# Macaron layers on one core: routing weights of a first-layer expert slot spread by one DMA instead of two, and the first group's spreading moved from the setup into the first pass

## What is computed

```
x = x + 0.5 * L0_ffn(layernorm(x))      # 16 experts of 64, 4 taken, and a shared expert
x = x + L0_attn(layernorm(x))           # causal softmax attention, 16 heads of 8
x = x + 0.5 * L0_ffn(layernorm(x))
x = x + 0.5 * L1_ffn(layernorm(x))      # 8 experts of 256, 2 taken
x = x + L1_attn(layernorm(x))           # gated, in blocks of 64, with a linear part
x = x + 0.5 * L1_ffn(layernorm(x))
```

```
h1 = einsum('td,eid->tei', xf, w1)
h3 = einsum('td,eid->tei', xf, w3)
h = silu(h1) * h3
y = einsum('tei,edi,te->td', h, w2, comb)    # comb[t, e]: the routing weight, 0 where not taken
```

## Time and profile before

| what | us |
|---|---|
| median of 3 runs | 1778.22 |
| lowest, highest | 1775.87, 1778.82 |
| the profiled execution, its own time | 1777.67 |
| its span in the trace | 1775.7 |

### The profile page before, as it was taken

The page is one execution under the profiler, slowest core; times in us unless marked ns, Lnnn a source line. Parts: engine busy times, 40 slices in busy tenths (PEclk is TensorE's granted clock), DMA queues, the critical chain, the costliest instruction groups (busy, mean ns, idle before and its releaser), DMA issues. The chain is left out here.

```text
span 1775.7 us, 25917 instructions
## 1 busy us (share of the span) xinstructions
PE 1644.0 (93%) x8360; PEld 1149.7 (65%) x8360; DVE 1289.3 (73%) x3879; ACT 1016.6 (57%) x1718; POOL 774.5 (44%) x734
## 2 busy tenths in 40 slices
PE   3999879899999999998999999999998988999998
PEld 2777645555555555554777767777777876777776
DVE  4777668788778878883777767777766876767775
ACT  3666415565566566566666645555555645555554
POOL 1566611311311311212566646555574615555555
PEclk9999969999999999999999999999999998999999
DMA  4222211011111111101233332111110002111120
GB/s 149 74 91 84 93 33 35 16 24 25 21 30 24 20 22 28 30 11 38 79 121 120 103 95 88 54 49 48 49 48 1 1 1 90 60 55 60 55 94 19
DMA packets 58246, 95.01 MB, mean 54 GB/s; under 512 B 9312, under 2 KB 17120, under 8 KB 58112
## 3 DMA queue, kind: packets, MB, share of 16 engines
q1 hardware_dynamic: 56000, 91.07, 18.2%
q10 hardware_dynamic: 2112, 2.30, 0.4%
HBM read 76.76 MB, written 2.88 MB: 45 GB/s over the span
## 5 line engine op out<-in xcount | busy, mean ns | idle before, releaser
L695 DVE TENSOR_TENSOR big<-banks,big 128x512 f32<-128x512 f32 x384 | 264.4, 689 | 214.7 <-ACT banks L632 179.8
L1157 ACT ACTIVATE big<-banks 128x1024 f32<-128x1024 f32 (+3 forms) x384 | 304.3, 810 | 187.9 <-PE banks L1068 182.5
L632 ACT ACTIVATE banks<-banks 128x512 f32<-128x512 f32 x384 | 224.0, 583 | 277.3 <-PE banks L575 272.1
L705 DVE TENSOR_TENSOR big<-big,banks 128x512 f32<-128x512 f32 x400 | 274.7, 687 | 29.8 <-PE banks L578 15.9
L1049 PE MATMUL banks<-arena 128*128 128x512 f32 (+3 forms) x768 | 251.9, 407 | 32.2 <-DVE att_mx L1285 15.4
L1285 DVE CUSTOM_DVE_ANT_0 banks<-banks,att_mask 128x128 f32<-128x128 f32 (+3 forms) x512 | 235.6, 521 | 52.2 <-PE banks L1049 51.6
L1197 POOL TENSOR_SCALAR_AFFINE_SELECT big<-big 128x512 f32<-128x512 f32 x128 | 81.2, 635 | 402.5 <-ACT big L1157 402.5
L1049 PEld LDWEIGHTS banks<-arena 128*128 128x128 f32 x768 | 136.6, 199 | 162.3 <-issue 98.2
L665 POOL TENSOR_TENSOR ffn1b_hid_l<-big,ffn1b_hid_h 128x512 fp32r<-128x512 f32 x128 | 165.5, 1293 | 128.3 <-ACT ffn1b_hid_h L637 128.3
L665 POOL TENSOR_TENSOR ffn1a_hid_l<-big,ffn1a_hid_h 128x512 fp32r<-128x512 f32 x128 | 165.2, 1291 | 118.0 <-ACT ffn1a_hid_h L637 118.0
L575 PE MATMUL banks<-xh,arena 128*128 128x512 f32 x512 | 208.7, 408 | 7.9 <-PEq L1451 6.8
(11 more groups left out here) (256 smaller groups left out, 3153.7 us busy)
## 6 DMA issues: line engine op xcount, KB each, us to landing
big<-weight_rows SPq DMA_DIRECT2D x256, 128.0 KB, 3.0
big<-weight_rows SPq DMA_DIRECT2D x128, 256.0 KB, 4.3
arena<-att_parts SPq DMA_DIRECT2D x16, 384.0 KB
arena<-att_parts SPq DMA_DIRECT2D x128, 48.0 KB
w_raw<-in_ffn_w_dram SPq DMA_DIRECT2D x12, 256.0 KB, 3.0
out_dram<-x SPq DMA_DIRECT2D x8, 256.0 KB, 2.3
setup_raw<-in_ffn_w_dram SPq DMA_DIRECT2D x3, 576.0 KB, 6.9
gau_angle<-in_consts_dram SPq DMA_DIRECT2D x2, 512.0 KB, 7.3
```

Source lines behind the costliest of these rows:

```text
L632: act.activation(gate if c < NSCALED else sil, gate, ACT.Silu).then_inc(silu_done, 1)
L695: dve.tensor_tensor(scl[:, num % 2, :], gate_ps[:, num % NB, :], share[:, c // PER, :], ALU.mult)\
L705: dve.tensor_tensor(hid[:, num % NH, :], scl[:, num % 2, :] if c < NSCALED else sil, up_ps[:, num % NB, :], ALU.mult).then_inc(hidden, 1)
L1157: act.activation(probs[:, unit % NPROB, 2 * pair:2 * pair + 2, 0:c], score_ps[:, pair, :, 0:c], ACT.Exp, scale=SCALE).then_inc(exped, 1)
```

## The change

Three edits, all around the filling of the slots in the first layer.

```diff
             later = lead.sync(sp, lambda g, e: None)
             later["rows"](lead.g0)
-            later["shares"](lead.g0)
...
                 free(g, e)
-                for h in range(r.HALVES):
-                    n, at = e * r.HALVES + h, h * P // r.HALVES
-                    sp.dma_start(r.share[at:at + P // r.HALVES, e, :],
-                                 k.rows[g % 2, n, :].partition_broadcast(P // r.HALVES)).then_inc(share_in[e], 16)
+                rows = k.rows[g % 2, e * r.HALVES:(e + 1) * r.HALVES, :]
+                sp.dma_start(r.share[:, e, :], rows.unsqueeze(1).broadcast_to([r.HALVES, P // r.HALVES, G]))\
+                  .then_inc(share_in[e], 16)
...
             def used(g, e):
-                sp.wait_ge(scaled, (g - 1) * NSCALED + (e + 1) * PER)
+                if g > g0:
+                    sp.wait_ge(scaled, (g - 1) * NSCALED + (e + 1) * PER)
...
             for g in range(g0, end):
                 if g > g0:
                     steps["rows"](g)
+                if g > g0 or r.spread_late:
                     steps["shares"](g)
-                elif ahead is not None:
+                if g == g0 and ahead is not None:
                     ahead.load_plain(sp)
...
                 if c % PER == 0:
-                    dve.wait_ge(share_in[c // PER], (g + 1) * HALVES * 16)
+                    dve.wait_ge(share_in[c // PER], (g + 1) * 16)
...
         ffn0a.router_in, ffn0a.router_count = ctx.enter_context(nc.semaphore("router_in")), 1
+        ffn0a.spread_late = True
```

More of the change, by code:

```diff
@@ L214, in routing @@
     r.end = r.g0 + NG
-    r.w, r.router_in, r.router_count = k.w[layer], None, 0
+    r.w, r.router_in, r.router_count, r.spread_late = k.w[layer], None, 0, False
     sems, own = k.moe_sems[layer], k.route_tiles[layer]
@@ L475, in phase_moe @@
     norm_done, comb_t, y_added, rows_out = r.norm_done, r.comb_t, r.y_added, r.rows_out
-    SLOTS, PER, NSCALED, HALVES = r.SLOTS, r.PER, r.NSCALED, r.HALVES
+    SLOTS, PER, NSCALED = r.SLOTS, r.PER, r.NSCALED
     LAG = 2
```

## The result

The changed kernel takes 2115.88 us (median; 2112.88 to 2121.31) against 1778.52 for the kernel before in the same comparison. The ratio is 1.190, with a 95% interval of 1.188 to 1.191: slower by 19%. The prediction was 2141, with a range of 2050 to 2310. The profiled execution took 2117.97 us with a span of 2115.5, 339.8 more than before.

A forecast was written before the change was run, and what follows sets the result against it. TensorE, busy 93% of the span, was taken to bound the kernel, with slots arriving just in time. Two-engine slots added +176.5 up to the attention and +186.8 in ffn0b, together +363 on 1777.7, giving 2141 us, range 2050 to 2310.

The forecast's parts named there:

- Two engines: First-layer slot DMA: the view read has outermost count 2, so two engines carry its 256 KB; chance 0.90.
- Time of a packet: Slot DMAs: 85 ns per 2 KB packet, bounds 75 and 104, so a slot takes 5.44 us.
- Fixed part and the chain between groups: First-layer passes: 2.3 us fixed from issue to landing; next group's slots issued 0.3 us after slot 7; period 46.1.
- ffn0a: First passes, before the attention: period 46.1 us, attention starting at 404.8, +176.5 including -9.0 from the setup.
- ffn0b: Passes after the attention: period 47.5 us, second layer starting at 1221.7 instead of 1034.93, +186.8.
- brings nothing: Attention's end: the 0.5 us wait there gains nothing, since the slots set the end of the pass behind it.
- worth nothing, since it waits: SyncE in the first layer: half as many DMAs to issue, some 5 us less a group, gains nothing.
- What would show it: Signs: 5472 small packets, L695 wait over 500 us, TensorE share about 77%, rows every 46 and 47.5, TensorE starting at 27.
- Second layer: Second-layer slot DMAs: an outermost count of one is most likely passed over, the same 16 engines, 0 us.
- The third rival: Second-layer slot DMAs confined to one engine by an outermost count of 1: about 2920 us; chance 0.03.
- The first rival: First-layer slot DMA runs over 16 engines, so the change does what it says: -9 to -15, 1767 us; chance 0.07.

The follow-up runs named there:

- The copies: Changed kernel with each row written eight times to HBM, a slot's DMA reading 16 rows by 8 repeats: 1815.2 us, ratio 1.021 to the kernel before.
- Eight copies: Changed kernel with the view turned to 64 by 2 by 512 and rows written eight times, only the first copy read: 1830.8 us, ratio 1.031.

## Why the prediction held, step by step

- **Two engines.** Right, to the packet (5472). Turned to sixteen, with the bytes and the two rows kept, the loss is gone. That what is read decides as well as what is written was read off four kinds of DMA in the trace of before; the same rule gave 4, 8 and 16 here.
- **Time of a packet.** Taken as 85 ns, measured 5.13 / 64 = 80 ns. The busy slices of the second layer were the better guide; why the packets were faster than the 104 ns with sixteen engines was not tried. 0.3 us a slot, 2.4 a group, makes 38 us over sixteen groups. This term, sized too large, is the main part of the miss of 25; smaller terms below went the other way.
- **Fixed part and the chain between groups.** The first group's slot 0 was used 7.7 us after its issue, as worked out. In group 1 it is 8.4 (79.43 against 71.01), 0.7 more. The write of the rows took 2.6 us (68.41 to 71.01) and ended with slot 7, so the next slots were issued 0.1 after slot 7 was used, as predicted to 0.2. The period is 43.9 instead of 46.1.
- **ffn0a**: forecast +176.5, measured +159.3; eight groups of 2.2 less. The tail from slot 7 to the attention is 387.54 - 378.28 = 9.3, as taken.

```profile
378.28 0.69 DVE L695 TENSOR_TENSOR big<-banks,big 128x512 f32<-128x512 f32 x1 [3.71 <-DMA big<-weight_rows]
```

- **ffn0b**: forecast +186.8, measured +178.9. The six periods from group 9's slots to group 15's are 45.3 instead of 47.5 ((1318.95 - 1047.21) / 6), -13. Against that stands the step that failed: group 9's slots were issued 53.1 us after group 8's (1047.21 - 994.13), not 47.5, +6. I had said that the attention's end "brings nothing" and that halving the DMAs on SyncE is "worth nothing, since it waits". In truth SyncE is held 30 us by issuing, inside the attention's block, so that the pass of group 8 starts at 1025 and then has to run its 22 us. I had treated issuing as half as long because there were half as many, while from the fourth DMA on each holds SyncE for 5.2 us on average (3.5 to 7.2), as long as the two engines take to carry one.
- **What would show it.** The wait of VectorE at L695 for `weight_rows` is 396.7 us and not over 500: 120 waits of 3.3, which is what VectorE's own work leaves of 5.13, and group 8 has none. TensorE's share is 83% and not 77%, since its busy time grew too, to 1756: with gaps in every chunk the granted clock fell to 0.77 in the first pass of ffn0a and 0.84 to 0.85 in the next, that is, they ran partly at the lower of the two levels (1.2 and 2.4 GHz). This did not set the time, since every `scale` of these passes waits for its slot. Rows were written every 43.9 us in ffn0a and 45.3 in ffn0b, and TensorE started at 27.35. Times from issue to landing are not given for these DMAs, so that sign could not be read.
- **Second layer**: unchanged, so an outermost count of one ahead of the 128 repeats does not confine. The third rival did not come.
- **The first rival's 1767**, had there been sixteen engines, is 1758 to 1763 in the runs. The move was sized right (9); the merging brought about 0.7 us in every pass of ffn0a, where I had allowed at most 6 in all.

The waits of VectorE (us in total, times, longest):

```profile
DVE big L695 <- DMA big<-weight_rows: 396.7, 120, 8.0
```

Three windows of the changed kernel show the clock. The columns are from and to, length, busy us of TensorE (count), its weight loads, VectorE, ScalarE and GpSimd, then granted clock, DMA share, GB/s.

```profile
27.00:71.00 44.00, 31.50 (x91) 21.79 (x92) 14.38 (x63) 12.85 (x24) 10.01 (x9) 0.77 0.13 49
71.00:115.00 44.00, 28.57 (x99) 19.65 (x99) 17.53 (x66) 13.62 (x27) 14.35 (x13) 0.84 0.13 49
...
1047.20:1092.80 45.60, 30.00 (x109) 21.33 (x107) 16.95 (x66) 14.00 (x28) 13.95 (x13) 0.85 0.16 58
```

## What to carry to other kernels

Before two DMAs are merged, look at the outermost count of what the merged one reads and of what it writes: here 2 by 64 by 512 ran on two engines, and 64 by 2 by 512 on sixteen, with the same bytes. The small packets on the page (one for each engine of a DMA) tell the number without any timing. And when slow DMAs stand in a row, the engine that issues them is held too (here from the third on), so a block that ends behind them ends later. The copies gave sixteen engines too, but left the kernel 57 us slower than turning the view did: a longer write that each pass waits for has its own price.

## What the runs showed of the hardware

- One DMA engine reads 2 KB rows from HBM at 80 ns each: two engines moved 51 GB/s and four 102, both flat, while sixteen reach eight times that (408) only for moments (401 to 434 in single slices of 0.25 us).
- Issuing is not free of the transfer. Of twelve slot DMAs issued between 27 and 76 us the shortest took 0.5 us of SyncE and the longest 7.2; the first two went in 0.7 and 0.5, the third in 2.8, the fourth took 5.2. With sixteen engines all eight went in 5.1.

```profile
L262 SPq DMA_DIRECT2D big<-weight_rows x12: 500/3450/7163, 27.3 to 75.6; - x12
```

- The write of the routing rows took 1.6, 2.3, 3.0 and 4.2 us for 32, 64, 128 and 256 KB, and stands in each pass's chain. Eight copies lengthened a pass of ffn0a from 22.5 to 26.9 us: 2.7 of landing, 0.7 of a later slot 0, and 1.0 behind it, where the granted clock was 0.94 instead of 1.00.
- Sixteen engines were slower with the rows 16 KB apart than with 2 KB, whether a DMA reads two rows (7.1 against 5.1 us to issue eight DMAs) or one row (6.5 against 3.7). Why was not tried.
